# Pooling the edge blocks one block later, with deeper rings, earlier row numbers and norms in steps

## The reference, cut to what matters

```
edge_index = stack([src, dst]); xn = layernorm(x)                     # x: 6250 nodes x 256
x = x + gnn(xn, edge_index, edge_weight) + mix(xn)                    # 100,000 edges, 4 heads of 64
x = x + ffn(layernorm(x))                                             # slices, attention over them, out
# gnn: feats = xn @ Ws + bs
#      w = exp(-relu((a_s[src] + a_d[dst] + aw_e * edge_weight + ab) / 20))
#      out = segment_sum(w * feats[dst], src) / segment_sum(w, src)
# mix: 4 layers of x += attention(layernorm(x)) (softmax of q over a head, of k over the nodes);
#      x += gelu(layernorm(x) @ W1 + b1) @ W2 + b2
```

## Time and profile before

| | us |
|---|---|
| median of 3 runs | 3684.2 |
| lowest, highest | 3680.34, 3685.38 |
| the profiled execution's own time | 3684.8 |
| its span in the trace | 3683.0 |
| PE busy | 3311.6 (90%) |
| DVE busy | 2372.1 (64%) |
| POOL busy | 1964.2 (53%) |
| ACT busy | 1162.7 (32%) |

### The profile page before, as it was taken

One profiled execution on the slowest core, in us unless ns is written; L12 is line 12 of the kernel. 1 busy time (PEld: TensorE's weight loads), 2 busy tenths in 40 slices (PEclk: granted clock), 3 DMA queues, 4 the chain that ended last, 5 costly groups with the idle time before them and its releaser, 6 DMA issues.

```text
span 3683.0 us, 43892 instructions
## 1 busy us (share of the span) xinstructions
PE 3311.6 (90%) x13948; PEld 2347.1 (64%) x13948; DVE 2372.1 (64%) x6185; ACT 1162.7 (32%) x2070; POOL 1964.2 (53%) x1745
## 2 busy tenths in 40 slices
PE   5888889999899999989997998888899987679979
PEld 3566556667667777757765666766666665455656
DVE  6887889944534444444457877766767765559941
ACT  2333233333333333323333333234334343212210
POOL 2110001777777777777765777747777776400000
PEclk8999999999999999999998999999999999889989
DMA  2322111222312222322234555545555557712134
GB/s 84 121 95 93 37 34 45 44 49 41 87 36 47 47 47 44 70 55 47 48 97 111 144 146 139 153 131 152 157 145 165 148 152 121 96 34 84 65 113 151
DMA packets 226435, 338.51 MB, mean 92 GB/s; under 512 B 52502, under 2 KB 180009, under 8 KB 225956
## 3 DMA queue, kind: packets, MB, share of 16 engines
q0 software_dynamic: 67840, 119.33, 17.0%
q1 hardware_dynamic: 120452, 161.93, 13.6%
q10 hardware_dynamic: 37920, 54.45, 4.8%
...
...
## 4 chain that ended last, share of the span: by engine, by line
PE 56%; DVE 24%; POOL 7%; DMA 6%; issue 5%; ACT 1%; DVEq 1%; SPq 0%; ACTq 0%
PE bank_v L1629 14%; PE bank_a L1614 11%; POOL arena L730 7%; PE bank_e L1671 6%; PE bank_v L1559 3%; PE bank_a L1531 3%; PE bank_v L1519 3%; PE bank_a L1461 3%; PE bank_v L1689 3%; PE bank_v L1602 3%; PE bank_v L1779 2%; DMA arena<-edge_weight_parts 2%; DMA arena<-gather_table,arena 2%; DVE arena L1093 2%; DVE st L965 2%
## 5 line engine op out<-in xcount | busy, mean ns | idle before, releaser
L761 POOL DMA_INDIRECT edge_records<-acc x800 | 969.6, 1212 | 621.1 <-issue 621.1
L730 POOL DMA_INDIRECT arena<-gather_table,arena x880 | 927.7, 1054 | 377.6 <-issue 258.9
L1629 PE MATMUL bank_v<-W_sb,gT 128*125 128x256 f32 x3200 | 748.8, 385 | 1.1 <-issue 1.1
L1614 PE MATMUL bank_a<-hT,W_sb 128*128 128x500 f32 (+1 forms) x1664 | 714.6, 577 | 4.2 <-issue 2.4
L1629 PEld LDWEIGHTS bank_v<-W_sb,gT 128*125 128x125 f32 x3200 | 593.3, 190 | 107.9 <-issue 24.1
L1671 PE MATMUL bank_e<-arena 128*125 128x260 f32 x1760 | 478.0, 418 | 83.6 <-DVE arena L1093 78.7
L1614 PEld LDWEIGHTS bank_a<-hT,W_sb 128*128 128x128 f32 x1664 | 318.6, 194 | 310.0 <-issue 291.1
L1671 PEld LDWEIGHTS bank_e<-arena 128*125 128x125 f32 x1760 | 334.6, 200 | 143.6 <-DVE arena L1093 91.8
L786 ACT ACTIVATE gT<-bank_a,cols 128x500 f32<-128x500 f32 (+1 forms) x416 | 275.0, 661 | 442.9 <-PE bank_a L1614 442.2
L786 ACT ACTIVATE hT<-bank_a,cols 128x500 f32<-128x500 f32 (+1 forms) x208 | 145.2, 748 | 501.5 <-PE bank_a L1461 483.7
L1093 DVE TENSOR_TENSOR arena<-arena 128x1024 f32<-128x1024 f32 x220 | 268.1, 1219 | 0.0
...
## 6 DMA issues: line engine op xcount, KB each, us to landing
residual<-xs SPq DMA_DIRECT2D x60, 500.0 KB
xs<-residual SPq DMA_DIRECT2D x60, 500.0 KB
arena<-edge_rows ACTq DMA_DIRECT2D x220, 125.0 KB
queries<-qT_out SPq DMA_DIRECT2D x48, 500.0 KB
qT_in<-queries ACTq DMA_DIRECT2D x39, 500.0 KB
...
edge_records<-acc POOLq DMA_INDIRECT x800
...
```

The source lines that it names most:

```text
L730: e.indirect_dma_start(g_of(j)[:, i, :], None, table_d, bass.IndirectOffsetOnAxis(ap=node[:, TE * j + i:TE * j + i + 1].bitcast(I32), axis ...
L761: e.indirect_dma_start(rec_d, bass.IndirectOffsetOnAxis(ap=pos_i[:, f:f + 1], axis=0), r3[:, f, :], None).then_inc(d_rec, 16)
L1614: o = e.matmul(b[:, 0:n], W[:, k, f * P:(f + 1) * P], hv[:, k, 0:n], start=k == 0, stop=k == KC - 1)
L1629: o = e.matmul(b[0:R, i % 2 * D:(i % 2 + 1) * D], gv[:, f, i * R:(i + 1) * R], W2_sb[:, f * D:(f + 1) * D], start=False, stop=f == FB - 1 ...
```

## The change

The sum of a block moves from PE's step j + 4 to step j + 5, and now waits for the one-hot instead of the weighing. The ring of gathered rows has 6 slots instead of 5, that of one-hots 2 instead of 5, that of row numbers 6 instead of 4. `one_hot` is made three half steps later, behind the weighing and behind `one_hot_T`. Row numbers are loaded at step k for block k + 3 instead of k + 1 (four blocks at step 0). POOL's gather k + 1 stays at step k and waits for the sum that PE makes in that step. There are 225 steps instead of 224. `normalise` becomes `moments`, `scale` and `apply`, and the latter two are put one or two PE stages later; `rsqrt` does its first two Newton steps in four chained instructions. `q_norm` is split into `q_sum` and the product, which now stands behind the second `attend`. SP loads the residual rows of the first two joins one group earlier.

```diff
@@ -65,13 +65,23 @@
 def feed_forward_up(l, s):
     for f in range(FB):
+        if f in (1, 2) and s >= 1 and l < LAST:
+            put(0.0, ("h1_scale", "h1_apply")[f - 1], l, s - 1)
...
-def feed_forward_down(l, s, i):
+def feed_forward_down(l, s, i, norm_beside=False):
...
+        if norm_beside:
+            put(0.0, ("ln2_scale", "ln2_apply")[h], l, s + 1)
+def norm(stage, l, s):
+    for part in (stage, stage + "_scale", stage + "_apply"):
+        put(0.0, part, l, s)
@@ -132,33 +144,41 @@
-        put(0.0, "ln2", l, 0)
+        norm("ln2", l, 0)
+put(0.0, "q_sum", l, END)
 put(0.0, "q_norm", l, END)
...
-put(0.0, "ln2", l, 1)
+norm("ln2", l, 1)
...
-            put(0.0, "q_norm", l + 1, s - 2)
+            put(0.0, "q_sum", l + 1, s - 2)
...
+        if l < LAST:
+            put(0.0, "q_norm", l + 1, s - 2)
...
     for i in range(tiles(s - 1)):
...
-        feed_forward_down(l, s - 1, i)
+        feed_forward_down(l, s - 1, i, i == 0 and 2 <= s < NGR)
...
-    put(0.0, "h1" if l < LAST else "total", *((l, s - 1) if l < LAST else (s - 1,)))
+    if l == LAST:
+        put(0.0, "total", s - 1)
+    elif s == NGR:
+        norm("h1", l, s - 1)
+    else:
+        put(0.0, "h1", l, s - 1)
@@ -191,9 +211,9 @@
-apart = room / (NB + 4)
+apart = room / (NB + 5)
...
-for k in range(NB + 4):
+for k in range(NB + 5):
@@ -295,9 +315,9 @@
-NG = 5
+NG, NO, NR = 6, 2, 6
...
-arena = sb("arena", [P, max(2 * SLOTS + NG * TE * (ROW + R) + 4 * BLK // 2, 8448 + PAIRS * GT * R)])
+arena = sb("arena", [P, max(2 * SLOTS + TE * (NG * ROW + NO * R) + NR * BLK // 2, 8448 + PAIRS * GT * R)])
@@ -659,6 +679,8 @@
     fetch_x(l + 1, s + 2 - NGR)
+elif s == PRE:
+    load_x(DEPTH + 1, 0, x_d[DEPTH % 2])
@@ -674,8 +696,8 @@
 store_x(DEPTH, s, x_d[DEPTH % 2])
...
-if s >= NGR - 2:
-    load_x(DEPTH + 1, s - (NGR - 2), x_d[DEPTH % 2])
+if s == PRE:
+    load_x(DEPTH + 1, 1, x_d[DEPTH % 2])
@@ -771,8 +793,8 @@
-elif 4 <= k < NB - 1:
-    e.wait_ge(e_full[1], k - 3)
+elif 5 <= k < NB - 1:
+    e.wait_ge(e_full[1], k - 4)
@@ -901,11 +923,11 @@
 k, = at
...
-for j in (range(2) if k == 0 else range(k + 1, min(k + 2, NB))):
-    if j >= 4:
-        e.wait_ge(e_full[0], j - 3)
-    e.dma_start(ohT_ring[j % 4][0:R, :], row_numbers(j)).then_inc(rows_in(j)[0], 16)
-    e.dma_start(ohT_ring[j % 4][R:P, :], weight_parts(j)).then_inc(rows_in(j)[0], 16)
+for j in (range(4) if k == 0 else range(k + 3, min(k + 4, NB))):
+    if j >= NR:
+        e.wait_ge(e_full[0], j - 5)
+    e.dma_start(ohT_ring[j % NR][0:R, :], row_numbers(j)).then_inc(rows_in(j)[0], 16)
+    e.dma_start(ohT_ring[j % NR][R:P, :], weight_parts(j)).then_inc(rows_in(j)[0], 16)
@@ -967,24 +989,28 @@
+def scale(nt, stats):
...
 def rsqrt(y, var, nt):
...
-    negh, a = nwt[0:R, 0:nt], nwt[0:R, 8:8 + nt]
+    negh, a, y15 = nwt[0:R, 0:nt], nwt[0:R, 8:8 + nt], nwt[0:R, 16:16 + nt]
...
-    for k in range(3):
-        step(e.tensor_tensor(a, y, y, ALU.mult))
-        step(e.tensor_tensor(a, a, negh, ALU.mult))
-        o = e.scalar_tensor_tensor(y, a, 1.5, y, ALU.add, ALU.mult)
-        if k < 2:
-            step(o)
-    return o
-def normalise(X, to, nt):
-    step(statistics(X, nt, st))
+    e.tensor_scalar(y15, y, 1.5, None, ALU.mult)
+    step(e.tensor_tensor(a, y, y, ALU.mult))
+    step(e.tensor_tensor(a, a, negh, ALU.mult))
+    step(e.scalar_tensor_tensor(a, a, 5.0 / 3.0, a, ALU.add, ALU.mult))
+    step(e.scalar_tensor_tensor(y, a, 1.25, y15, ALU.add, ALU.mult))
+    step(e.tensor_tensor(a, y, y, ALU.mult))
+    step(e.tensor_tensor(a, a, negh, ALU.mult))
+    return e.scalar_tensor_tensor(y, a, 1.5, y, ALU.add, ALU.mult)
+def apply(X, to, nt):
@@ -1094,13 +1121,13 @@
 def one_hot(j):
-    e.tensor_tensor(oh_ring[j % NG].rearrange("p (t r) -> p t r", t=TE),
+    e.tensor_tensor(oh_ring[j % NO].rearrange("p (t r) -> p t r", t=TE),
...
 def one_hot_T(j):
...
-    e.tensor_scalar(ohT_ring[j % 4][0:R, :], ohT_ring[j % 4][0:R, :], iota_part[0:R, :], None, ALU.is_equal)\
+    e.tensor_scalar(ohT_ring[j % NR][0:R, :], ohT_ring[j % NR][0:R, :], iota_part[0:R, :], None, ALU.is_equal)\
@@ -1222,6 +1249,10 @@
+elif stage == "q_norm":
+    l, s = at
+    qa = qn_of(s)[:, 0:tiles(s) * D].rearrange("p (a d) -> p a d", d=DH)
+    sm = qst[0:R, 0:tiles(s) * HM]
@@ -1266,7 +1297,12 @@
-    normalise(by_tile(x_of(l + 1, s)[:, :]), by_tile(h2b[:, :]), tiles(s)).then_inc(h2_set, 1)
+    moments(by_tile(x_of(l + 1, s)[:, :]), tiles(s), st)
+elif stage in ("ln2_scale", "h1_scale"):
+    step(scale(tiles(at[1]), st))
+elif stage == "ln2_apply":
+    l, s = at
+    apply(by_tile(x_of(l + 1, s)[:, :]), by_tile(h2b[:, :]), tiles(s)).then_inc(h2_set, 1)
@@ -1318,16 +1357,16 @@
-    if k < 4:
+    if k < 5:
...
-if k >= 4:
-    if k > NB + 2:
-        e.wait_ge(e_done[1], k - 4)
+if k >= 5:
+    if k > 5:
+        e.wait_ge(e_done[1], k - 5)
     for h in range(2):
...
-            e.wait_ge(e_full[1], k - 3)
+            e.wait_ge(e_full[1], k - 4)
@@ -1335,16 +1374,18 @@
     weigh(k - 3)
+if 4 <= k <= NB + 3:
...
-              for i in (2 * (k - 3), 2 * (k - 3) + 1)]
+              for i in (2 * (k - 4), 2 * (k - 4) + 1)]
...
-    one_hot(k)
...
+if k >= 3:
+    one_hot(k - 3)
@@ -1657,18 +1700,18 @@
-        o = e.matmul(ps_as[:, i * 3 * HG:(i + 1) * 3 * HG], ohT_ring[j % 4][:, i * P:(i + 1) * P],
+        o = e.matmul(ps_as[:, i * 3 * HG:(i + 1) * 3 * HG], ohT_ring[j % NR][:, i * P:(i + 1) * P],
...
-    if k < 4:
+    if k < 5:
...
-if k >= 4:
-    j = k - 4
-    e.wait_ge(p_set, j + 1)
+if k >= 5:
+    j = k - 5
+    e.wait_ge(oh_set, j + 1)
     for h in range(2):
...
-            o = e.matmul(ps_sum[h], oh_ring[j % NG][:, i * R:(i + 1) * R], g_of(j)[:, i, :],
+            o = e.matmul(ps_sum[h], oh_ring[j % NO][:, i * R:(i + 1) * R], g_of(j)[:, i, :],
```

30 lines of the change are left out of this document (19 added, 11 removed).

## The result

| | before | changed |
|---|---|---|
| median, us | 3682.27 (4 runs) | 3653.01 (4 runs) |
| lowest, highest | 3676.19, 3685.38 | 3646.88, 3655.80 |
| profiled execution, and its span | 3684.8, 3683.0 | 3646.88, 3645.1 |

The ratio of the changed kernel to the kernel before is 0.992, with a 95% interval of 0.9901 to 0.9939: 29 us faster, where 42 were forecast. The profiled execution of the changed kernel is the shortest of its four, so the spans differ by 37.9 us, more than the medians do.

A forecast was written before the change was run, and what follows sets the result against it. POOL's gathers were taken to set the pace of the edge stretches. The terms, 8 + 14 + 0 + 8 + 9 + 4 = 43 us, taken from 3684.8 gave 3641.8, say 3642 us; range 3598 to 3670.

The forecast's parts named there:

- (c): Second edge stretch: 117 blocks stay at 5.48 us each, so 0 us gained; ends -3 and +20.
- (a): Norms in fewer and separate steps, before the layers, in the first layer and at layer changes: 8 us gained.
- (b): Pooling one block later with a ring of six, first edge stretch and pauses: 14 us gained, ends 5 and 20.
- (d): The end, 3085 to 3237 us: row numbers asked for three blocks ahead gain 8 us, ends -10 and 25.
- below 20: Sign that the forecast is right: DVE's 47.4 us of waits for row loads falls below 20.
- rows first, then the gathers: Forecast order of the waits at the end: for row numbers first, then for the gathers themselves; no size given.
- need the DMA engines anyway: At the end, 16 blank blocks occupy the DMA engines regardless: 124 us from 3085 us to the last landing.
- (e): First join: residual rows asked for about one group earlier, so PE's 9.21 us wait goes: 9 us gained.
- (f): Eleven further joins: PE's wait of 0.64 us each falls by 0.33: 4 us gained, ends 1 and 6.
- The stalls pay: Rival: gathers fall to halfway between 1.370 and 1.249 us, giving 48 us more, 3594 us; chance 0.14.
- Only shifted: Rival: DMA engines alone bound the end and later pooling gives the extra block only, 3682 us; chance 0.08.
- Norm pieces stuck behind edge steps: Rival: in edge layers, norms' scale and apply queue on DVE behind edge steps; 3688 to 3733 us; chance 0.06.

The follow-up runs named there:

- change_again: The changed kernel run once more, unaltered: 3656.23 us against 3684.04 for the kernel before, ratio 0.9925.
- no_weighing: The changed kernel weighing only the first of each head's 64 columns of a gathered row: 3580.59 us, ratio 0.9729 to the kernel before.
- no_one_hot: The changed kernel without making one-hots after the first two (a one-column write instead): 3632.64 us, ratio 0.9863 to the kernel before.
- rows_one_ahead: The changed kernel with row numbers loaded one block ahead instead of three: 3776.95 us, ratio 0.9838, on a chip where the kernel before took 3840.33.
- blank_spread: The changed kernel with blank records' node numbers spread over the table instead of all 0: 3744.35 us against 3840.33 for the kernel before, ratio 0.9763.

## Why the prediction came out as it did

**The direction, the bound and the size of five terms were right.** The forecast's main reading, that the gathers' 5.48 us a block bound the second stretch and PE's 97 us of waits there were no prize, held: PE's wait on the weighing went and the time of the stretch stayed. That is term (c), forecast as 0 (blocks 88 to 203 came 1.4 us later in the first trace); in change_again it is below 0, because that execution's mean gather is 16 ns longer (16 ns x 4 x 116 blocks = 7 us).

**(a), 8 us: right** in sum, 8.3 in one trace and 5.0 in that of change_again. Inside it something was against it that the forecast called free: the split q_norm. "q_norm lies 4 us ahead of q_t" was true of the edge stretches, but in the first layer, where the sort stands in DVE's queue, PE waited 13.2 us for it instead of 3.7, and 4.6 us of the lead were lost. The norms gave more than was put down: at the 150th matmul `bank_v<-h,ek`, ahead of that loss, the lead was 9.4 us (6.0 in change_again).

**(b), 14 us: wrong, and the only large miss.** Its steps were right one by one: 7 to 9 us of POOL's waits on PE went, and one block more is gathered before the pause. The step that failed is the silent one, that the gathers keep their length while POOL's waits go. They became 46 ns longer in the first stretch: 8.8 us of waits and 5.5 us of a block ahead of the pause on one side, 14 us of longer gathers on the other. The forecast had the rule in hand: the Trainium skill, GPSIMD Engine Reference, section 1 (Specifications), says that GpSimd shares its SBUF interfaces with VectorE and contends with VectorE instructions that have two SBUF inputs. The weighing and the one-hot are such, and no_weighing and no_one_hot bear it out: 1088 to 995 and to 1061 ns. The trace agrees on the two inputs: beside a DVE instruction with one input in SBUF and one in PSUM 119 gathers took 946 ns. The rule was applied only to the question whether gathers would quicken, with the words that the change "only moves" such instructions. Where they lie when a gather starts is just what costs. It is not that more of them came to lie beside gathers: in blocks 6 to 83 the weighing and the one-hot overlapped gathers for 121.0 us before and 118.2 after. But 105 of the 312 gathers now start within one of them instead of 98, with 566 ns of it left on average instead of 465, and these average 1387 ns instead of 1268: 105 x 0.44 - 98 x 0.32 = 15 us. The other 207 take 947 ns, against 953 before. With the pooling undone it is 97 gathers, 511 ns and 1334 ns. Which of the other parts brought gathers and weighing into that step was not tried.

**(d), 8 us: 11 measured, the right cause by another path.** The earlier row loads are what gave it, as rows_one_ahead shows. But the sum let half of POOL's 26.7 us of waits come back and took one step off, and POOL's waits stayed, at 24.9 us. The gathers of the last 16 blocks start within 110.4 us, against 108.6 before. The gain lies behind the last gather, from 39.7 us to 26.9 until the last pooling matmul: before, two of DVE's waits for rows fell there, at 3201.80 us (10.06) and 3214.81 us (9.48), and now none does. That 8 and 11 lie near each other is luck. DVE's wait for rows fell to 20.5 us, which missed "below 20" narrowly. The order "rows first, then the gathers" is reversed: the first wait for a gather ends at 3086 us and the first for rows at 3129 us, and the gathers' are the larger, 40.0 us. That the blank blocks "need the DMA engines anyway" is what kept the gathers' time there as it was, and is a matter of the padding alone: blank_spread shows about half of the engines' time for more bytes a second when the rows don't all come from one row.

**(e), 9 us: right**, 9.9; the first join's addition has no wait before it any more. **(f), 4 us: 7.3.** PE's waits for a join in 3300 to 3400 us, 3.2 us for 5, became

```profile
PE bank_a L1504 <- DVE h L1015: 1.5, 5, 0.3
```

which is 0.34 us less each, as the 0.33 forecast; from the third group to the last the lead grew by 3.2 us. The rest lies ahead of these joins: 1.2 us in the first group's slice logits, 0.3 in the long wait for the second join (9.64 us before, 9.30 now, as good as unchanged, as forecast), and 2.6 in the second group behind it. Of PE's timeline there, first before, then changed:

```profile
3292.35 1.93 PE L1461 MATMUL bank_a<-ident,h 125*128 125x125 f32 x8 [9.64 <-DVE h L989]
3294.21 3.75 PE L1689 MATMUL bank_v<-Wqkv,hT 128*125 128x512 f32 x4
...
3298.50 3.77 PE L1689 MATMUL bank_v<-Wqkv,hT 128*125 128x512 f32 x4
```

```profile
3262.83 1.93 PE L1504 MATMUL bank_a<-ident,h 125*128 125x125 f32 x8 [9.30 <-DVE h L1015]
3264.69 3.24 PE L1732 MATMUL bank_v<-Wqkv,hT 128*125 128x512 f32 x4
...
3268.22 1.98 PE L1732 MATMUL bank_v<-Wqkv,hT 128*125 128x512 f32 x4
```

The same four matmuls take 3.75 us or 1.98, and before the change two such groups behind the wait were long, now part of one. The granted clock was 0.58 from 3292 to 3304 us before the change and 0.82 from 3263 to 3275 us after it: most of the one stretch at the lower of the clock's two levels (1.2 GHz), most of the other at 2.4 GHz, both behind 9 to 10 us in which PE had nothing to do. Ahead of that wait it had been 0.80 and 1.00. The forecast had no term for what PE's clock gives back behind a wait.

**The rivals.** "The stalls pay" (3594) did not happen, since the gathers became longer. "Only shifted" (3682) was right about the pooling, and right that the gathers of the end would keep their time, and wrong about what follows the last gather and about the rest. "Norm pieces stuck behind edge steps" is not seen: in 1958 to 3082 us PE waited 5.9 us for a norm, twice.

The sum of the measured leads is 37.9 us in one pair of executions, 29 between the medians. The difference is within what the gathers and the stages ahead of them do from one execution to the next. Against the forecast's 43 us it is term (b), 14 us, that is missing, and (d) and (f) gave some 6 us more than was put down.
